# The MLP's product silu(gate)*up made by VectorE from PSUM in a decoder layer

## The chip, the cores and the metric

The kernel runs on one core of a Trainium2 chip. The metric is the device time of one execution in microseconds (us), as the median of several runs; a profile shows one execution instruction by instruction. The engines are TensorE (PE; its weight loads are PEld), VectorE (DVE), ScalarE (ACT) and GpSimd (POOL), with SyncE (SP) issuing the transfers. Each engine runs its own queue in order, and an instruction starts once the semaphores that it names have reached their values.

## What is computed

A decoder layer over x of 8 batches x 256 tokens x 512 features in three residual parts, each followed by a layer norm. Cut to what matters:

```python
# 1: gated linear recurrence
i, f, g = x @ Wi.T, x @ Wf.T, x @ Wg.T
a = sigmoid(f); b = silu(i) * (1 - a)
h = linear_scan(a, b); xg = h * silu(g)
x = layernorm(x + (xg * rsqrt(mean(xg**2) + eps) * w_norm) @ Wo.T)
# 2: WKV recurrence over the keys x and the values ctx, along the tokens
x = layernorm(x + wkv(w, u, k=x, v=ctx))
# 3: MLP, I = 1408, weights and activations rounded to 255 levels by row (quant)
gate, up = quant(x) @ quant(W_gate_up).T          # 1408 columns each
h = silu(gate) * up
x = layernorm(x + quant(h) @ quant(W_down).T)
```

## The kernel before

A batch is two tiles of 128 tokens; tile n = 2b + t is token half t of batch b, 16 tiles in all. The first part of the time loads, rounds and turns the weights. Then the three parts are overlapped across batches: one pass of the loop (`iteration(b, par)`, passes b = 1 to 5) does the MLP of batch b, the WKV part of batch b+1 and the gated recurrence of batch b+2. Batch 0's MLP stands before the loop, those of batches 6 and 7 after it. Nothing schedules the instructions: each engine's `iteration` is an order written out by hand, with semaphores between the engines.

The MLP of a tile is cut in three chunks c of 512, 512 and 384 columns (`CHUNKS`). For each:

- `mlp_up` (TensorE, L557) multiplies into a slot of PSUM, `slot_ps[:, s]`, the gate in its first bank and up in its second. There are two slots, s = (t + c) % 2.
- `scale_products` (VectorE) multiplies the gate by the weights' scales into `gate_buf` (L1522, counted by `gate_scaled`) and up by its scales into `hid_buf(t)` (L1525, counted by `mlp_read`). Both buffers are rows of `ring` in SBUF. After the second the slot is free.
- `silu` (ScalarE, L867) works in place in `gate_buf`.
- `hidden` (GpSimd, L1189) multiplies `hid_buf` by `gate_buf` in place and counts `hid_ready`.
- `hidden_max` (VectorE, L1534) takes the row's largest magnitude; after the third chunk `hidden_scale` derives the scale.

Then `round_hidden` (ScalarE), `turn_hidden` (TensorE, L577, transposes into slot (t+1+NC) % 2), `read_hidden` (ScalarE, into `hqT`), `mlp_down` (TensorE, L590, into slot (t+NC) % 2), `read_down` (VectorE, L1567), `residual_3` (GpSimd, L1194) and layer norm.

TensorE's uses of the slots wait by the count `mlp_read`: `mlp_up`'s chunk 2 for the same tile's chunk 0; `turn_hidden(n)` for tile n+1's chunk 1 (L574, `chunks_read(n) - 1`); `mlp_down(n)` for tile n+1's chunk 2 (L586, `chunks_read(n)`). In a pass TensorE's queue goes, in its second half: `mlp_up` of tile (b,1) chunk 1 and chunk 2, `turn_values` (L523), `turn_hidden(2b)`, `project_out(b+2, 0)` (L455), `sum_squares(b+2)`, `project_out(b+2, 1)`, `mlp_down(2b)`, `turn_inputs(b+1)` (L532); and the next pass begins with `mlp_up` of batch b+1, which waits for ScalarE's `read_inputs` (L858, `xqT`) of what `turn_inputs` wrote. VectorE's `mean_square(b+2)` (L1384) waits for `sum_squares`, `scale_2(b+1)` stands behind it and gives the scale that ScalarE's `round_2` needs ahead of `turn_inputs`.

## Time and profile before

| | |
|---|---|
| median of 3 runs | 489.2 us (488.76 to 492.02) |
| span of the profiled execution | 485.3 us |
| VectorE busy | 426.4 us, 88% |
| TensorE busy | 376.6 us, 78% |
| ScalarE busy | 290.8 us, 60% |
| GpSimd busy | 277.5 us, 57% |
| `hidden` on GpSimd (L1189) | 66.2 us in 48 instructions |

The page's map of the span in 40 slices shows VectorE at eight or nine tenths of nearly every slice from the middle on. The three stages are the weights (to about 106 us), the overlapped passes (batch 0's MLP from 106 us, the loop's five passes from 156 to 417 us) and the batches 6 and 7 after the loop. A row of a timeline gives start, duration and, in brackets, the engine's idle time ahead of it with what ended it; the row of the next instruction on VectorE often starts 0.08 us before the end of the one ahead. Line numbers are those of the kernel before.

### The profile page before, as it was taken

How to read it: one execution, taken by the hardware profiler on the slowest of the kernel's cores; microseconds unless marked ns; L12 is line 12 of the kernel's file. 1: busy time of each engine (PE TensorE's matmuls, PEld its weight loads, DVE VectorE, ACT ScalarE, POOL GpSimd, SP SyncE). 2: the span in 40 equal slices, each digit the busy share in tenths (PEclk: the TensorE clock that was granted, in tenths of full speed). 3: DMA queues.
4: the chain of work that ended last, by engine and by line, in shares of the span. 5: the costliest groups of instructions: out<-in, count | busy, mean ns of one | idle time of the engine just before them, and what ended most of it. 6: DMA issues, size and time to landing. Idle time of an engine off the chain costs nothing.

```text
span 485.3 us, 7425 instructions
## 1 busy us (share of the span) xinstructions
PE 376.6 (78%) x2484; PEld 285.2 (59%) x2484; DVE 426.4 (88%) x705; ACT 290.8 (60%) x374; POOL 277.5 (57%) x249
## 2 busy tenths in 40 slices
PE   5977972997098995899598977898689959556782
PEld 4965972886064973588365865396459836223331
DVE  3897599848999999989998999799998999999983
ACT  4766673493446965387547864586538654854752
POOL 4546574706836754586365935384558636763643
PEclk8997895999589997999989989899799988976998
DMA  8849441460110010201002010301020101000001
GB/s 312 300 171 141 149 156 53 132 108 35 50 37 1 0 66 1 102 8 54 14 22 88 1 66 0 109 0 65 0 105 3 65 0 42 24 0 22 22 24 66
DMA packets 13340, 31.70 MB, mean 65 GB/s; under 512 B 4864, under 2 KB 4864, under 8 KB 13312
## 3 DMA queue, kind: packets, MB, share of 16 engines
q1 hardware_dynamic: 13312, 31.35, 20.4%
q8 instruction: 15, 0.25, 0.2%
q14 instruction: 13, 0.11, 0.1%
HBM read 27.14 MB, written 4.21 MB: 65 GB/s over the span
## 4 chain that ended last, share of the span: by engine, by line
DVE 45%; PE 17%; issue 16%; POOL 9%; DMA 8%; ACT 4%; DVEq 1%; POOLq 0%; SPq 0%; ACTq 0%
DVE q_state L1427 7%; PE proj_ps L455 6%; PE slot_ps L557 6%; DVE p_state L1439 6%; DVE hid_max L1534 4%; DMA ring<-w_gate_up_dram 3%; POOL q_state L1173 2%; DVE ring L1522 2%; DVE ring L1525 2%; DVE num L1447 2%; DVE row_max L1591 2%; DVE inp L1359 2%; POOL ring L1189 2%; POOL z L1194 2%; PE slot_ps L590 2%
## 5 line engine op out<-in xcount | busy, mean ns | idle before, releaser
L557 PE MATMUL slot_ps<-w1q,xqT 128*128 128x512 bf16 (+1 forms) x384 | 88.2, 382 | 20.6 <-DVE z L1567 12.9
L1189 POOL TENSOR_TENSOR ring<-ring 128x512 f32<-128x512 f32 (+1 forms) x48 | 66.2, 1386 | 18.8 <-ACT ring L867 18.7
L557 PEld LDWEIGHTS slot_ps<-w1q,xqT 128*128 128x128 bf16 x384 | 37.8, 102 | 63.8 <-issue 14.5
L455 PE MATMUL proj_ps<-x_high,proj_high 128*128 128x256 f32 x384 | 64.3, 289 | 5.0 <-DVE proj_low L1350 1.9
L455 PE MATMUL proj_ps<-x_high,proj_low 128*128 128x256 f32 x384 | 61.5, 282 | 0.0
L455 PE MATMUL proj_ps<-x_low,proj_high 128*128 128x256 f32 x384 | 61.1, 281 | 0.0
L455 PEld LDWEIGHTS proj_ps<-x_high,proj_high 128*128 128x128 f32 x384 | 52.9, 189 | 7.8 <-issue 6.0
L867 ACT ACTIVATE ring<-ring,zero_bias,x_scale 128x512 f32<-128x512 f32 (+1 forms) x48 | 36.9, 772 | 31.7 <-DVE ring L1522 31.6
L455 PEld LDWEIGHTS proj_ps<-x_high,proj_low 128*128 128x128 f32 x384 | 52.6, 190 | 0.0
L455 PEld LDWEIGHTS proj_ps<-x_low,proj_high 128*128 128x128 f32 x384 | 52.4, 190 | 0.0
L523 PE MATMUL turn_ps<-identity,num 128*128 128x128 f32 x64 | 14.5, 391 | 44.2 <-DVE num L1465 44.2
L1194 POOL TENSOR_TENSOR z<-z,x 128x512 f32<-128x512 f32 x16 | 22.4, 1398 | 44.5 <-DVE z L1567 44.5
L874 ACT ACTIVATE ring<-ring,round_bias,hid_inv 128x768 f32<-128x768 f32 (+1 forms) x32 | 30.2, 967 | 25.9 <-DVE hid_inv L1556 25.9
L590 PE MATMUL slot_ps<-w2q,hqT 128*128 128x512 bf16 x176 | 41.9, 388 | 4.0 <-ACT hqT L881 3.1
L1522 DVE TENSOR_TENSOR ring<-slot_ps,scale_rows 128x512 f32<-128x512 f32 (+1 forms) x48 | 30.7, 640 | 13.3 <-PE slot_ps L557 13.3
L1122 POOL TENSOR_SCALAR ring<-ring,row_inv 128x512 f32<-128x512 f32 (+1 forms) x26 | 28.3, 1100 | 19.1 <-DVE row_inv L1597 19.1
L523 PEld LDWEIGHTS turn_ps<-identity,num 128*128 128x128 f32 x64 | 10.6, 197 | 47.6 <-DVE num L1465 47.4
L1439 DVE TENSOR_TENSOR_SCAN p_state<-decay_col,p_state 128x256 f32<-128x256 f32 x32 | 34.4, 1118 | 4.1 <-POOL p_state L1151 4.0
L1427 DVE TENSOR_TENSOR_SCAN q_state<-decay_col,q_state 128x256 f32<-128x256 f32 x32 | 36.8, 1209 | 0.0
L1151 POOL TENSOR_TENSOR p_state<-q_state,c_sb 128x512 f32<-128x512 f32 x16 | 21.0, 1312 | 20.0 <-ACT q_state L822 11.3
L590 PEld LDWEIGHTS slot_ps<-w2q,hqT 128*128 128x128 bf16 x176 | 16.2, 99 | 24.7 <-issue 5.6
L1591 DVE TENSOR_REDUCE row_max<-ring 128x2 f32<-128x1024 f32 (+1 forms) x15 | 19.7, 1316 | 12.3 <-DMA ring<-w_gate_up_dram 11.4
(115 smaller groups left out, 904.7 us busy)
## 6 DMA issues: line engine op xcount, KB each, us to landing
ring<-w_gate_up_dram SPq DMA_DIRECT2D x11, 512.0 KB, 4.9
forget<-xT_dram SPq DMA_DIRECT2D x8, 512.0 KB, 3.3
x_sb<-x_dram SPq DMA_DIRECT2D x8, 512.0 KB, 3.4
c_sb<-cT_dram SPq DMA_DIRECT2D x8, 512.0 KB, 4.9
out_dram<-z SPq DMA_DIRECT2D x16, 256.0 KB, 2.1
ring<-w_down_dram SPq DMA_DIRECT2D x4, 704.0 KB, 5.0
x<-wfT_dram SPq DMA_DIRECT2D x2, 512.0 KB, 5.0
x<-woT_dram SPq DMA_DIRECT2D x2, 512.0 KB, 4.6
```

The costliest lines, as they stand in the source:

```text
L455: last = nc.tensor.matmul(out, a, b, start=(i == 0), stop=(i == len(terms) - 1))
L557: last = nc.tensor.matmul(slot_ps[:, s, half * 512:half * 512 + width], xqT[:, par, d, t * P:(t + 1) * P], w1q[:, d, half * I + at:half * ...
L590: last = nc.tensor.matmul(slot_ps[:, s, 0:D], hqT[:, i, :], w2q[:, i, :], start=(i == 0), stop=(i == IB - 1))
L867: nc.scalar.activation(g, g, ACT.Silu, bias=zero_bias[:, :], scale=x2_scale[:, par, t:t + 1]).then_inc(silu_ready, 1)
L874: nc.scalar.activation(h, h, ACT.Identity, bias=round_bias[:, :], scale=hid_inv[:, t:t + 1]).then_inc(hid_rounded, 1)
L1122: last = nc.gpsimd.tensor_scalar(rows[:, a, :], rows[:, a, :], row_inv[:, c:c + 1], ROUND, ALU.mult, ALU.add)
L1189: nc.gpsimd.tensor_tensor(hid, hid, gate_buf[:, at:at + width], ALU.mult).then_inc(hid_ready, 1)
L1194: nc.gpsimd.tensor_tensor(z3[:, t, :], z3[:, t, :], x2[:, par, t, :], ALU.add).then_inc(z3_ready, 1)
L1427: last = nc.vector.tensor_tensor_scan(e_past[:, c, :], decay_col[:, c:c + 1].to_broadcast([P, T]), e_past[:, c, :], 0.0, ALU.mult, ALU.add)
L1439: last = nc.vector.tensor_tensor_scan(ev_past[:, c, :], decay_col[:, c:c + 1].to_broadcast([P, T]), ev_past[:, c, :], 0.0, ALU.mult, ALU.add)
L1522: nc.vector.tensor_tensor(gate_buf[:, at:at + width], slot_ps[:, s, 0:width], scale_rows[:, at:at + width], ALU.mult).then_inc(gate_scaled, 1)
L1591: nc.vector.tensor_reduce(row_max[:, cols], rows, AX.X, ALU.max, apply_absolute_value=True).then_inc(row_max_ready, 1)
```

## The change

The product moves from GpSimd to VectorE. `scale_products` now writes the scaled up half back into its PSUM slot and counts `up_scaled`. A new VectorE step `hidden` reads that slot and `gate_buf` and writes `hid_buf`; it counts `mlp_read`, so that the slot is free, by every wait on `mlp_read`, after the product and no longer after the scaling. `hidden_max` waits on `mlp_read`. GpSimd's `hidden` and its 48 calls are gone. The new calls are placed by hand in VectorE's order, a few other VectorE steps change places, and ScalarE does one `silu` ahead of `read_hidden` in two places outside the loop.

```diff
-                        wait(dve, hid_ready, n * NC)
-                        wait(dve, hq_turned, 2 * n - 2)
+                        wait(dve, mlp_read, n * NC)
...
-                    nc.vector.tensor_tensor(hid_buf(t)[:, at:at + width],
+                    nc.vector.tensor_tensor(slot_ps[:, s, 512:512 + width],
                                             slot_ps[:, s, 512:512 + width],
                                             scale_rows[:, I + at:I + at + width],
-                                            ALU.mult).then_inc(mlp_read, 1)
+                                            ALU.mult).then_inc(up_scaled, 1)
+
+            def hidden(b, t, c):
+                n = b * TB + t
+                at, width = CHUNKS[c]
+                s = (t + c) % 2
+                dve.wait_ge(silu_ready, n * NC + c + 1)
+                dve.wait_ge(up_scaled, n * NC + c + 1)
+                if c == 0:
+                    wait(dve, hq_turned, 2 * n - 2)
+                nc.vector.tensor_tensor(hid_buf(t)[:, at:at + width],
+                                        slot_ps[:, s, 512:512 + width],
+                                        gate_buf[:, at:at + width],
+                                        ALU.mult).then_inc(mlp_read, 1)
...
@@ -1608,20 +1586,23 @@
                 n = b * TB
                 scale_products(b, 0, [0])
                 scale_products(b, 0, [1])
-                scale_products(b, 0, [2])
                 hidden_max(b - 1, 1, 0)
                 hidden_max(b - 1, 1, 1)
                 hidden_max(b - 1, 1, 2)
+                hidden(b, 0, 0)
+                hidden_scale(b - 1, 1 - par, 1)
                 sum_values(b + 1, 0)
-                hidden_scale(b - 1, 1 - par, 1)
+                scale_products(b, 0, [2])
                 numerator(b + 1, 0)
                 hidden_max(b, 0, 0)
                 layer_norm_3(n - 2, 0)
+                hidden(b, 0, 1)
                 hidden_max(b, 0, 1)
                 sum_weights(b + 1, 0)
                 sum_weights(b + 1, 1)
+                normalise_3(n - 2, 0)
+                hidden(b, 0, 2)
                 hidden_max(b, 0, 2)
-                normalise_3(n - 2, 0)
...
                 refine(b + 1, 0)
                 refine(b + 1, 1)
+                hidden(b, 1, 0)
                 gating(b + 2)
                 scale_products(b, 1, [1])
...
                 scale_products(b, 1, [2])
+                hidden(b, 1, 1)
                 normalise_2(b + 1, 1 - par)
                 mean_square(b + 2)
                 scale_2(b + 1, 1 - par)
+                hidden(b, 1, 2)
                 normalise_3(n - 1, 1)
```

**VectorE, second half of a pass**, from the `gating` product `inp` to the first `residual_1` (`slot_ps` is the MLP's two slots, `num` the WKV result, `msq` the mean square that TensorE sums). Before:

```order
L1373 TENSOR_TENSOR inp<-inp,gate 128x1024 [waits proj_read]
...
L1522 TENSOR_TENSOR ring<-slot_ps,scale_rows 128x512 [waits mlp_done]
L1525 TENSOR_TENSOR ring<-slot_ps,scale_rows 128x512
L1378 TENSOR_TENSOR xg_low<-inp,xg_high 128x1024 [waits xg_high_ready]
L1471 TENSOR_TENSOR num<-x1,turn_ps 128x512 [waits y_turned] x2
...
L1485 TENSOR_SCALAR ve2<-mv2 128x2 [waits rstd2_ready,mv2_ready]
...
L1522 TENSOR_TENSOR ring<-slot_ps,scale_rows 128x384 [waits mlp_done]
L1525 TENSOR_TENSOR ring<-slot_ps,scale_rows 128x384
L1492 TENSOR_SCALAR x2<-num,mv2,rstd2 128x512 [waits z3_ready,rstd2_ready]
...
L1384 TENSOR_SCALAR msq<-turn_ps 128x2 [waits rms_ready,sumsq_done]
L1499 TENSOR_REDUCE x2_max<-x2 128x2 [waits x2_ready]
```

And after:

```order
L1503 TENSOR_TENSOR ring<-slot_ps,ring 128x512 [waits hq_turned]
...
L1339 TENSOR_TENSOR inp<-inp,gate 128x1024 [waits proj_read]
...
L1487 TENSOR_TENSOR ring<-slot_ps,scale_rows 128x512 [waits mlp_done]
L1490 TENSOR_TENSOR slot_ps<-slot_ps,scale_rows 128x512
L1344 TENSOR_TENSOR xg_low<-inp,xg_high 128x1024 [waits xg_high_ready]
L1437 TENSOR_TENSOR num<-x1,turn_ps 128x512 [waits y_turned] x2
...
L1451 TENSOR_SCALAR ve2<-mv2 128x2 [waits rstd2_ready,mv2_ready]
...
L1490 TENSOR_TENSOR slot_ps<-slot_ps,scale_rows 128x384
L1503 TENSOR_TENSOR ring<-slot_ps,ring 128x512 [waits up_scaled,silu_ready]
...
L1350 TENSOR_SCALAR msq<-turn_ps 128x2 [waits rms_ready,sumsq_done]
...
L1470 TENSOR_SCALAR x2_scale<-x2_max 128x2 [waits hid_inv_ready,silu_ready,x2_max_ready]
...
L1503 TENSOR_TENSOR ring<-slot_ps,ring 128x384 [waits up_scaled,silu_ready]
```

What counts `mlp_read` for chunk 1 was the third row before (L1525, right behind the gating product); now it is the second `ring<-slot_ps,ring 128x512`, behind the split of the states, two residuals, a layer norm's statistics and chunk 2's scaling.

**TensorE, the same half pass**, in the change (its instructions and their waits are the same in both kernels; `w1q` are the up weights, `w2q` the down weights, `xg` the gated states):

```order
L557 MATMUL slot_ps<-w1q,xqT 128x384 [waits mlp_read]
L557 MATMUL slot_ps<-w1q,xqT 128x384 x7
...
L523 MATMUL turn_ps<-identity,num 128x128 [waits e_now_ready,msq_ready,e_past_ready,y_ready]
...
L577 MATMUL slot_ps<-identity16,ring 128x128 [waits mlp_read]
...
L455 MATMUL proj_ps<-wo_high,xg_high 128x512 [waits proj_read]
...
L488 MATMUL turn_ps<-ones,gate 128x1 [waits z2_ready,sq_sum_ready]
...
L590 MATMUL slot_ps<-w2q,hqT 128x512 [waits hq_ready,mlp_read]
...
L532 MATMUL turn_ps<-identity16,num 128x128 [waits z2_ready,x2_rounded]
```

Nothing moved on this queue; what moved is the VectorE instruction that its three waits on `mlp_read` are for.

## Rows read from the trace of the kernel before

**Rows 1.** The page: the span, then busy us (share of the span) xinstructions by engine.

```profile
span 485.3 us, 7425 instructions
...
PE 376.6 (78%) x2484; PEld 285.2 (59%) x2484; DVE 426.4 (88%) x705; ACT 290.8 (60%) x374; POOL 277.5 (57%) x249
```

**Rows 2.** Busy us by engine (x instructions) over the loop's five passes.

```profile
sum 261.20, PE 223.04 PEld 168.83 DVE 245.09 ACT 162.52 POOL 154.81; mean PE 44.61 PEld 33.77 DVE 49.02 ACT 32.50 POOL 30.96
```

**Rows 3.** The page: groups by line, busy us, mean ns | idle us before, releaser.

```profile
L1189 POOL TENSOR_TENSOR ring<-ring 128x512 f32<-128x512 f32 (+1 forms) x48 | 66.2, 1386 | 18.8 <-ACT ring L867 18.7
...
L1522 DVE TENSOR_TENSOR ring<-slot_ps,scale_rows 128x512 f32<-128x512 f32 (+1 forms) x48 | 30.7, 640 | 13.3 <-PE slot_ps L557 13.3
```

**Rows 4.** Timeline, VectorE, first half of pass 3: start us, us, instruction.

```profile
258.22 0.69 DVE L1522 TENSOR_TENSOR ring<-slot_ps,scale_rows 128x512 f32<-128x512 f32 x1 [0.46 <-PE slot_ps L557]
...
269.89 1.15 DVE L1451 COPY num<-c_sb 128x2 f32<-128x2 f32 x1
...
273.30 5.26 DVE L1427 TENSOR_TENSOR_SCAN q_state<-decay_col,q_state 128x256 f32<-128x256 f32 x4
...
278.93 1.28 DVE L1583 TENSOR_SCALAR z<-z,mv,rstd 128x512 f32<-128x512 f32 x1
280.13 1.26 DVE L1439 TENSOR_TENSOR_SCAN p_state<-decay_col,p_state 128x256 f32<-128x256 f32 x2
...
282.95 0.17 DVE L1451 COPY num<-c_sb 128x2 f32<-128x2 f32 x1
...
288.00 0.68 DVE L1522 TENSOR_TENSOR ring<-slot_ps,scale_rows 128x512 f32<-128x512 f32 x1
```

**Rows 5.** Timeline, GpSimd, the same half pass.

```profile
267.63 3.38 POOL L1189 TENSOR_TENSOR ring<-ring 128x512 f32<-128x512 f32 x2
...
273.47 1.33 POOL L1189 TENSOR_TENSOR ring<-ring 128x384 f32<-128x384 f32 x1
274.75 1.66 POOL L1158 TENSOR_TENSOR num<-e_now,c_sb 128x512 f32<-128x512 f32 x1
276.36 1.65 POOL L1164 TENSOR_TENSOR q_state<-q_state,e_now 128x512 f32<-128x512 f32 x1
...
278.64 1.28 POOL L1164 TENSOR_TENSOR q_state<-q_state,e_now 128x512 f32<-128x512 f32 x1
```

**Rows 6.** Timeline, VectorE, second half of that pass.

```profile
295.07 0.68 DVE L1525 TENSOR_TENSOR ring<-slot_ps,scale_rows 128x512 f32<-128x512 f32 x1
...
300.60 0.54 DVE L1525 TENSOR_TENSOR ring<-slot_ps,scale_rows 128x384 f32<-128x384 f32 x1
301.06 1.94 DVE L1492 TENSOR_SCALAR x<-num,mv,rstd 128x512 f32<-128x512 f32 x2
```

**Rows 7.** Timeline, TensorE, second half of that pass [idle before <-releaser].

```profile
287.54 4.88 PE L557 MATMUL slot_ps<-w1q,xqT 128*128 128x512 bf16 x16 [2.45 <-DVE z L1567]
...
295.81 0.79 PE L577 MATMUL slot_ps<-identity,ring 128*128 128x128 f16 x11 [1.68 <-DVE ring L1525]
297.23 1.20 PE L455 MATMUL proj_ps<-wo_high,xg_high 128*128 128x512 f32 x4 [0.63 <-DVE xg_low L1378]
...
303.37 2.55 PE L590 MATMUL slot_ps<-w2q,hqT 128*128 128x512 bf16 x11
306.73 0.62 PE L532 MATMUL turn_ps<-identity,num 128*128 128x128 f16 x8 [0.81 <-ACT num L851]
```

**Rows 8.** Timeline: first up matmuls of pass 3 (TensorE), xqT of pass 4 (ScalarE).

```profile
256.19 3.62 PE L557 MATMUL slot_ps<-w1q,xqT 128*128 128x512 bf16 x16 [1.28 <-ACT xqT L858]
...
307.39 1.11 ACT L858 ACTIVATE xqT<-turn_ps,half_bias 128x1024 bf16<-128x1024 f16 x1 [0.71 <-PE turn_ps L532]
```

**Rows 9.** Busy us by engine in three stretches, granted clock (PEclk), DMA.

```profile
256.00:260.00 4.00, 3.81 (x20) 1.98 (x21) 3.08 (x6) 0.81 (x2) 0.69 (x1) 1.00 0.52 194
287.50:290.90 3.40, 3.36 (x10) 1.34 (x11) 3.40 (x4) 1.96 (x3) 3.33 (x3) 0.60 0.00 0
308.60:312.10 3.50, 3.45 (x9) 1.25 (x10) 1.88 (x4) 1.15 (x1) 1.47 (x2) 0.51 0.59 225
```

**Rows 10.** Timeline, VectorE, end of tile 1, before the loop.

```profile
152.40 3.69 DVE L1416 TENSOR_SCALAR x<-inp,mv,rstd 128x512 f32<-128x512 f32 x2
156.01 0.68 DVE L1522 TENSOR_TENSOR ring<-slot_ps,scale_rows 128x512 f32<-128x512 f32 x1
```

**Rows 11.** Timeline after the loop: TensorE, tiles 12 and 13; VectorE, tile 14.

```profile
446.87 0.77 PE L577 MATMUL slot_ps<-identity,ring 128*128 128x128 f16 x11 [0.17 <-DVE ring L1525]
...
460.25 1.02 PE L590 MATMUL slot_ps<-w2q,hqT 128*128 128x512 bf16 x4 [0.80 <-ACT hqT L881]
...
455.57 0.69 DVE L1522 TENSOR_TENSOR ring<-slot_ps,scale_rows 128x512 f32<-128x512 f32 x1
...
458.44 0.54 DVE L1583 TENSOR_SCALAR z<-z,mv,rstd 128x512 f32<-128x512 f32 x1
```

More of the change, by code:

```diff
@@ L1046, in _ @@
             round_2(1, 1, 1)
+            silu(0, 0, 1, [1])
             read_hidden(0, 0, 0)
             read_hidden(0, 0, 1)
-            silu(0, 0, 1, [1])
             read_inputs(1, 1)
@@ L1080, in _ @@
             round_hidden(12, 0, 1)
+            silu(6, 0, 1, [1])
             read_hidden(12, 0, 0)
             read_hidden(12, 0, 1)
-            silu(6, 0, 1, [1])
             silu(6, 0, 1, [2])
@@ L1180, in rstd_2 @@
                                         ALU.pow).then_inc(rstd2_ready, 1)
-            def hidden(b, t, chunks=range(NC)):
-                n = b * TB + t
-                for c in chunks:
-                    at, width = CHUNKS[c]
-                    pool.wait_ge(silu_ready, n * NC + c + 1)
-                    pool.wait_ge(mlp_read, n * NC + c + 1)
-                    hid = hid_buf(t)[:, at:at + width]
-                    nc.gpsimd.tensor_tensor(hid, hid, gate_buf[:, at:at + width],
-                                            ALU.mult).then_inc(hid_ready, 1)
             def residual_3(n, par, t):
@@ L1208, in iteration @@
                 now_values(b + 1, 0)
-                hidden(b, 0, [0])
-                hidden(b, 0, [1])
                 past_values(b + 1, 1)
                 rstd_3(n - 2, 0)
-                hidden(b, 0, [2])
                 now_values(b + 1, 1)
@@ L1281, in _ @@
             denominator(1, 1)
-            hidden(0, 0, [0])
             newton(1, 0)
             newton(1, 1)
-            hidden(0, 0, [1])
-            hidden(0, 0, [2])
             sum_blocks(2)
@@ L1289, in _ @@
             rms_scale(2)
-            hidden(0, 1, [0])
-            hidden(0, 1, [1])
             rstd_1(2)
-            hidden(0, 1, [2])
             iteration(1, 1)
@@ L1305, in _ @@
             past_values(7, 1)
-            hidden(6, 0, [0])
-            hidden(6, 0, [1])
             now_values(7, 1)
-            hidden(6, 0, [2])
             denominator(7, 0)
@@ L1532, in hidden_max @@
                 at, width = CHUNKS[c]
-                dve.wait_ge(hid_ready, n * NC + c + 1)
+                dve.wait_ge(mlp_read, n * NC + c + 1)
                 nc.vector.tensor_reduce(hid_max[:, c:c + 1], hid_buf(t)[:, at:at + width], AX.X,
@@ L1719, in _ @@
             weigh_inputs(2)
+            hidden(0, 0, 0)
             numerator(1, 1)
@@ L1727, in _ @@
             gating(2)
+            hidden(0, 0, 1)
             residual_2(1, 0)
@@ L1732, in _ @@
             split_states(2)
+            hidden(0, 0, 2)
             hidden_max(0, 0, 2)
@@ L1739, in _ @@
             scale_products(0, 1, [1])
+            hidden(0, 1, 0)
+            scale_products(0, 1, [2])
             mean_square(2)
-            scale_products(0, 1, [2])
+            hidden(0, 1, 1)
             residual_1(2, 0)
             residual_1(2, 1)
+            hidden(0, 1, 2)
             layer_norm_1(2)
@@ L1760, in _ @@
             hidden_scale(5, 1, 1)
-            scale_products(6, 0, [2])
+            hidden(6, 0, 0)
             sum_values(7, 0)
             sum_values(7, 1)
+            scale_products(6, 0, [2])
             numerator(7, 0)
             hidden_max(6, 0, 0)
+            hidden(6, 0, 1)
             sum_weights(7, 0)
@@ L1768, in _ @@
             hidden_max(6, 0, 1)
+            hidden(6, 0, 2)
             hidden_max(6, 0, 2)
@@ L1781, in _ @@
             layer_norm_2(7)
+            hidden(6, 1, 0)
             scale_products(6, 1, [1])
@@ L1785, in _ @@
             scale_2(7, 1)
+            hidden(6, 1, 1)
             layer_norm_3(11, 1)
@@ L1788, in _ @@
             hidden_max(6, 1, 1)
+            hidden(6, 1, 2)
+            hidden_max(6, 1, 2)
             read_down(12, 6, 0)
-            hidden_max(6, 1, 2)
             hidden_scale(6, 0, 1)
@@ L1795, in _ @@
             normalise_3(11, 1)
+            hidden(7, 0, 0)
+            normalise_3(12, 0)
+            hidden(7, 0, 1)
             scale_products(7, 0, [2])
-            normalise_3(12, 0)
             hidden_max(7, 0, 0)
             hidden_max(7, 0, 1)
+            hidden(7, 0, 2)
             hidden_max(7, 0, 2)
@@ L1804, in _ @@
             scale_products(7, 1, [1])
+            hidden(7, 1, 0)
             hidden_max(7, 1, 0)
+            hidden(7, 1, 1)
             scale_products(7, 1, [2])
@@ L1808, in _ @@
             hidden_max(7, 1, 1)
+            hidden(7, 1, 2)
             hidden_max(7, 1, 2)
```

14 lines of the change are left out of this document (1 added, 13 removed).

## The prediction

> **What bounds the kernel now.** The page's first part comes first: VectorE is busy 426.4 of 485.3 us, TensorE 376.6, GpSimd 277.5 [rows 1]. An average hides stages, so the stretches of the loop come next: its five passes last 261.2 us together, 52.2 each, and VectorE is busy 49.0 of a mean pass [rows 2]. In the loop VectorE is the bound, almost without a gap. TensorE waits for it: 2.45 us for `read_down`, then 1.68 us for the scaling of up chunk 1 of the odd tile, which ends at 295.75 (295.07 + 0.68), and `turn_hidden` starts at 295.81 [rows 6, 7]. That last wait is by `mlp_read`, the count whose meaning is changed. From there to the next pass TensorE works through two projections, `mlp_down` and `turn_inputs`, with time left over: `turn_inputs` waits 0.81 us for ScalarE's `num`, which waits for VectorE [rows 7].
>
> **The change: VectorE's time.** 48 instructions leave GpSimd (66.2 us there) and 48 come to VectorE [rows 3]. No row has a product of a PSUM and an SBUF row of `ring`, but the scaling has the same shape, one operand from PSUM and one from SBUF: 0.64 us each in the mean, of which 0.08 lies under the next instruction (300.60 + 0.54 against 301.06) [rows 3, 6]. That makes 48 x 0.56 = 27 us. A pass has six of them, four of 512 columns at 0.60 and two of 384 at 0.46 (300.60 to 301.06): 3.3 us. Writing the scaled row to PSUM in place of SBUF I cost at nothing; no row shows such a write, and a tenth of a microsecond on each of six would be 0.6 us a pass, inside the range.
>
> Something comes back. Instructions on VectorE are held by GpSimd's: the copy of two columns at 269.89 takes 1.15 us and ends at 271.04, where two `hidden` end (267.63 + 3.38 = 271.01); the same copy at 282.95, with GpSimd idle, takes 0.17 [rows 4, 5]. Four scans take 5.26 us beside `hidden` chunk 2, `now_values` and a `denominator`, against 1.26 for two that are free; the normalisation behind them takes 1.28 [rows 4, 5], against 0.54 at 458.44, where it is free [rows 11]; the two at 301.06 take 1.94, so one of those is held too, by about 0.9 [rows 6]. By their GpSimd partners I put down to `hidden` 0.98 (copy), some 0.8 (the first held scan, beside the GpSimd row at 273.47), 0.9 (the pair at 301.06) and, for the small instructions between, an estimated 0.6: 3.3 us a pass. So VectorE's own sum is even: +3.3 - 3.3.
>
> The Trainium skill has a rule for this, SBUF — State Buffer, section "Who interferes with whom": GpSimd and a VectorE instruction with two SBUF inputs, or in a two-port mode, exclude each other for the whole instruction, and one with at most one SBUF input does not contend. The trace agrees with the copy and the scans, and by the rule the new product, one input from PSUM, is not held itself. By it the sum is the even one above.
>
> In the first half of a pass I pushed the rows. Product 0 and `hidden_scale` fall where chunk 2's scaling stood and where VectorE waited; products 1 and 2 add 1.07 us and 0.1 of handoffs; the copy gives back 0.98, and of the 2.8 + 0.74 us that scans and normalisation are held, some 1.9 stay (`now_values` and one `denominator` still run there), so 1.6 goes. Net -1.4: tile (b,1)'s first scaling, 29.8 us behind the pass's first (258.22 to 288.00) [rows 4], comes 28.4 us behind it.
>
> **The change: the slot is held longer.** This decides. `turn_hidden(2b)` waits for tile (b,1)'s chunk 1. Its release was the scaling of up at 295.75. It is now product 1, which stands where the row at 301.06 stands; product 0 ahead of it adds 0.60, its own duration is 0.68, and the -1.4 comes off: 301.06 + 0.60 + 0.68 - 1.4 = 300.9 [rows 6]. The release comes 5.2 us later in the pass, 42.7 us behind the pass's first scaling. (In every other pass the first half is 1.3 us shorter, so I take 42.1.) Queued behind `turn_hidden` on TensorE are both `project_out`, `sum_squares`, `mlp_down` and `turn_inputs`. VectorE itself soon waits for them, at `mean_square`, with `scale_2` behind it, `round_2` behind that.
>
> From the release to the next pass's first scaling, from rows: `turn_hidden` 0.75; projections and sum 303.37 - 297.23 = 6.14; `mlp_down` 2.55; `turn_inputs` 0.62; ScalarE's `xqT` 1.11 [rows 7, 8]; chunk 0's matmuls from their start at 256.19 to the scaling at 258.22, 2.03 [rows 4, 8]; handoffs 0.1. That is 13.3. VectorE's path beside it is shorter. Counted from the release, `msq` runs at +4.2, when `sum_squares` is done; the row scale takes it to +6, product 2 to +6.5 (`mlp_down` could start at +6.9); the residuals, layer norm, `read_down` and `normalise_1` end by +12. So a pass takes 42.1 + 13.3 = 55.4 at the full clock, +3.2 on 52.2.
>
> **TensorE's clock.** After the 2.45 us pause the granted clock is 0.60 in the next 3.4 us, and in another stretch it is 0.51, the 1.2 GHz level: 9 matmuls in 3.45 us, where the full level did 20 in 3.81 [rows 7, 9]. Ahead of the new release TensorE pauses some 5.6 us (the odd tile's chunk 2 and `turn_values` are done by about 295.3). So `turn_hidden` and the first projection fall in a slow stretch of 3.4 us at least; half its work is lost, 1.7 us. Lower bound 0, upper bound 3.4 (two stretches). The skill's TensorE: Matmul & The Clock Gate, Part 1, states the same two levels and that the gate lowers the clock after idleness; this rule speaks against any change that makes TensorE wait. The loop then costs 5 x (3.2 + 1.7) = 24.5 us, from 16 to 33.
>
> **Before and after the loop.** Batch 0: chunk 2 of tile 0 waits for product 0, and the last two `project` behind it on TensorE delay `gating` by 1.7 us; chunk 1 of tile 1 waits for product 2 of tile 0 (0.8 more); `silu` of chunk 2 stands behind `read_hidden`, which waits for product 1, so product 2, `mlp_down` and `read_down` come some 3.5 us late. Against them the normalisation at 152.40, 3.69 us long where about 1.0 is free, is no longer held [rows 10]. Pushed through, the first scaling of pass 1 moves from 156.0 to 160 or 162: +5, from 2 to 7.
>
> Batches 6 and 7: `turn_hidden(12)`, at 446.87, moves behind product 1 of tile 13, +4.6, and `mlp_down(12)` behind product 2, whose `silu` stands behind `read_hidden`, +0.9; 1.0 less from scans no longer held: +4.5. Tile 14: `mlp_down(13)` started 4.7 us behind the tile's first scaling (455.57 to 460.25) [rows 11]; it now needs product 2, which by the new order ends at about +8: +3. Tile 15 has the same shape but ends in the row scale: +2. Together +9.5, from 5 to 12.
>
> **Sum.** 24.5 + 5 + 9.5 = 39 us on the profiled 485.3, or 524.3. The median of the runs is 3.9 above that execution, so 528.2; the terms' ends give 23 to 52, so 512 to 541.
>
> **Rivals.**
> - *No change.* VectorE stays the bound, the sum of its time is even, and TensorE's later start is absorbed: 489 (484 to 494). For it: [rows 2], and the gain in the first half. Against it: a chain of 13.3 us behind a release 42.1 us into a pass of 52.2 doesn't fit, by 3.2. It decides if the release comes that much earlier or the chain is that much shorter. 4%.
> - *Faster.* More comes back than I count: if all 48 `hidden` held VectorE for their 1.39 us, 66 us would come back for 27. It decides once more than 27 us come back and the chain fits: 2 us a pass less, 479. By the Trainium skill's GPSIMD Engine Reference, section 4.1, elementwise work with two inputs belongs on VectorE, being about twice as fast there; the rows have 1.39 against 0.64 [rows 3]. Against it: GpSimd isn't the bound, and [rows 4] shows less than 3.5 us a pass held by `hidden`. 3%.
> - *VectorE's time alone.* It stays the bound and nothing comes back: 489.2 + 27 = 516. The held instructions would have to be held as long by what GpSimd still does. 8%.
> - *The chain with a slow clock throughout*, both projections and `mlp_down` at the lower level: 4 us more a pass, 548. 7%.
> - *My forecast*, the later release: 78%.
>
> **How the numbers follow.** The time is the sum, 528. The range 512 to 541 takes in the terms' ends and the rival at 516. About 1% is what a measurement of this kernel tells from no change: faster 0.03, same 0.04, slower 0.93.
>
> **What would show it.** In the profile after: passes of 56 to 58 us; VectorE's busy share down to about 82%, with a new wait of 3 to 5 us at `msq` for TensorE's `turn_ps`; TensorE idle 5 to 6 us ahead of `turn_hidden`, released by the new product; a granted clock near 0.5 behind it; the copies at 0.17 us more often. Wrong would be: a `turn_hidden` released by something other than the product; a pass under 54 us (the chain has slack that I don't see); products held by GpSimd, well over 0.68 us each.

## The result and the profile after

The changed kernel takes 539.6 us (median; 537.8 to 540.9), the kernel before 490.6 beside it: ratio 1.101 (1.095 to 1.106), 49 us slower. Line numbers are now those of the changed kernel: L1487 and L1490 scale gate and up, L1503 is the product, L1350 `mean_square`, L1545 `read_down`. The page's head, and groups with the idle time before them and its releaser:

```profile
span 538.0 us, 7379 instructions
...
PE 383.9 (71%) x2462; PEld 294.1 (55%) x2484; DVE 423.9 (79%) x753; ACT 291.6 (54%) x374; POOL 212.6 (40%) x201
...
L557 PE MATMUL slot_ps<-w1q,xqT 128*128 128x512 bf16 (+1 forms) x377 | 86.6, 378 | 61.4 <-DVE ring L1503 53.4
...
L577 PE MATMUL slot_ps<-identity,ring 128*128 128x128 f16 x176 | 16.7, 261 | 39.4 <-DVE ring L1503 38.5
L1503 DVE TENSOR_TENSOR ring<-slot_ps,ring 128x512 f32<-128x512 f32 (+1 forms) x48 | 30.7, 639 | 4.6 <-ACT ring L867 4.6
```

VectorE has 48 instructions more and is busy 2.5 us less than before [rows 1]; they cost 30.7 us and more than that came back. But its share falls from 88 to 79 per cent: it now waits. TensorE is idle for 92 us (53.4 + 38.5) in these two groups until a product frees a slot, where it was idle for 33 us (20.6 + 12.4) ahead of the same two before, for any reason:

```profile
L557 PE MATMUL slot_ps<-w1q,xqT 128*128 128x512 bf16 (+1 forms) x384 | 88.2, 382 | 20.6 <-DVE z L1567 12.9 <-ACT xqT L858 7.6
...
L577 PE MATMUL slot_ps<-identity,ring 128*128 128x128 f16 x176 | 15.6, 245 | 12.4 <-DVE ring L1525 6.9 <-ACT ring L874 4.6 <-DVE z L1567 0.8
```

VectorE in pass 3 (start, duration, instruction, idle time before it with its releaser):

```profile
280.29 0.69 DVE L1487 TENSOR_TENSOR ring<-slot_ps,scale_rows 128x512 f32<-128x512 f32 x1 [1.42 <-PE slot_ps L557]
...
290.53 0.17 DVE L1417 COPY num<-c_sb 128x2 f32<-128x2 f32 x1
...
294.31 3.49 DVE L1393 TENSOR_TENSOR_SCAN q_state<-decay_col,q_state 128x256 f32<-128x256 f32 x4
...
307.14 0.69 DVE L1487 TENSOR_TENSOR ring<-slot_ps,scale_rows 128x512 f32<-128x512 f32 x1
...
320.68 0.68 DVE L1503 TENSOR_TENSOR ring<-slot_ps,ring 128x512 f32<-128x512 f32 x1
321.28 1.00 DVE L1458 TENSOR_SCALAR x<-num,mv,rstd 128x512 f32<-128x512 f32 x2
327.94 0.16 DVE L1350 TENSOR_SCALAR msq<-turn_ps 128x2 f32<-128x2 f32 x1 [5.66 <-PE turn_ps L488]
...
336.87 0.69 DVE L1487 TENSOR_TENSOR ring<-slot_ps,scale_rows 128x512 f32<-128x512 f32 x1 [1.44 <-PE slot_ps L557]
```

And TensorE behind the release at 321.36 (320.68 + 0.68):

```profile
321.42 1.35 PE L577 MATMUL slot_ps<-identity,ring 128*128 128x128 f16 x11 [5.85 <-DVE ring L1503]
322.53 2.05 PE L455 MATMUL proj_ps<-wo_high,xg_high 128*128 128x512 f32 x4
...
327.77 1.17 PE L455 MATMUL proj_ps<-wo_high,xg_high 128*128 128x512 f32 x4
```

The pass is 56.6 us long: 41.1 to the release, 15.5 from there to the next pass's first scaling. `turn_hidden` took 0.79 for the same 11 matmuls in pass 3 before [rows 7]; here it and most of the first projection run at half speed. The windows of the two stretches (columns as in rows 9; the last but two is the granted clock) show that it is the clock:

```profile
321.40:326.90 5.50, 5.48 (x21) 4.56 (x22) 0.88 (x2) 2.18 (x3) 0.00 (x0) 0.50 0.00 0
327.00:334.00 7.00, 6.57 (x37) 4.35 (x36) 5.85 (x14) 1.84 (x3) 0.99 (x2) 1.00 0.28 88
```

The half clock itself is not new. Rows 7 show the one pass of the kernel before in which this work ran at full speed; in the other four it took the same 1.33 to 1.36 and 2.05 to 2.07 us as here. Its pass 4:

```profile
348.64 1.35 PE L577 MATMUL slot_ps<-identity,ring 128*128 128x128 f16 x11 [1.22 <-DVE ring L1525]
350.06 2.07 PE L455 MATMUL proj_ps<-wo_high,xg_high 128*128 128x512 f32 x4
```

What is new is that the pass now waits behind it, as e5_busy and e7_before_busy show below.

Cut at the first scaling of a batch, the time of each kernel's profiled execution divides as follows. "Batch 0" is from the first scaling of all to that of pass 1, "pass" the mean of the loop's five, then batch 6 to batch 7, and batch 7 to the end of VectorE's last instruction.

Each ratio is to runs of the kernel before on the same chip at the same time.

| kernel | median, us | ratio to before | batch 0 | pass | b6 to b7 | b7 to end |
|---|---|---|---|---|---|---|
| before | 490.6 | | 50.1 | 52.3 | 38.3 | 27.0 |
| the change | 539.6 | 1.101 (1.095 to 1.106) | 58.5 | 56.3 | 46.9 | 38.0 |
| e1_sbuf | 504.6 | 1.032 (1.027 to 1.036) | 51.5 | 52.7 | 42.2 | 32.6 |
| e2_sbuf_late | 549.5 | 1.124 (1.119 to 1.128) | 58.6 | 58.6 | 47.7 | 36.8 |
| e3_pe_order | 521.5 | 1.068 (1.062 to 1.073) | 58.4 | 53.9 | 46.9 | 34.2 |
| e5_busy | 521.7 | 1.068 (1.060 to 1.075) | 57.9 | 54.2 | 44.6 | 33.4 |
| e6_place | 519.5 | 1.062 (1.057 to 1.067) | 58.7 | 51.7 | 47.1 | 36.7 |
| e7_before_busy | 490.7 | 1.000 (0.997 to 1.003) | 50.4 | 52.1 | 37.7 | 27.0 |
| e8_orders | 506.5 | 1.032 (1.028 to 1.037) | 56.1 | 50.9 | 46.5 | 36.8 |
| e9_order_alone | 494.9 | 1.010 (1.006 to 1.014) | 51.3 | 51.9 | 40.2 | 29.0 |
| e10_loop_only | 487.1 | 0.993 (0.990 to 0.997) | 50.7 | 51.4 | 38.6 | 26.8 |
| e11_orders_before | 501.8 | 1.026 (1.022 to 1.031) | 50.7 | 54.1 | 38.6 | 27.0 |

So the change costs 8.5 us in batch 0, 19.9 in the loop and 19.6 behind it. The stretch ahead of the first scaling, where the change alters nothing, took 105.9 us in the profiled execution of before and 108 to 111 in all others; together with the 1.8 us by which a span is shorter than the time of the same execution, that accounts for this span, 485.3, lying below the median. The last stretch also varies: the change, e3_pe_order and e6_place have the same instructions in it, and it took 38.0, 34.2 and 36.7 us. The granted clock over it was 0.86, 0.95 and 0.86. Differences of a few us there are not an experiment's doing by this table alone.

### The profile page after: what moved, and what is told of

It reads as the page before. It is cut to its first block, busy times and chain, and to the rows that moved or that the text cites. A ratio compares the mean times of both kernels' runs of the same rounds, so it can differ in the third digit from the quotient of the medians.

```text
span 538.0 us, 7379 instructions
## 1 busy us (share of the span) xinstructions
PE 383.9 (71%) x2462; PEld 294.1 (55%) x2484; DVE 423.9 (79%) x753; ACT 291.6 (54%) x374; POOL 212.6 (40%) x201
## 3 DMA queue, kind: packets, MB, share of 16 engines
q1 hardware_dynamic: 13312, 31.35, 19.6%
## 4 chain that ended last, share of the span: by engine, by line
DVE 39%; PE 30%; issue 14%; DMA 7%; ACT 5%; POOL 4%; DVEq 1%; POOLq 0%; SPq 0%; ACTq 0%
PE proj_ps L455 14%; PE slot_ps L557 8%; DVE q_state L1393 5%; PE slot_ps L590 5%; DVE ring L1503 4%; DMA ring<-w_gate_up_dram 4%; DVE p_state L1405 4%; DVE slot_ps L1490 3%; DVE hid_max L1512 3%; DVE num L1431 2%; DVE inp L1325 2%; DVE row_max L1569 2%; DVE ring L1487 2%; DVE stats L1443 2%; PE slot_ps L577 2%
## 5 line engine op out<-in xcount | busy, mean ns | idle before, releaser
L557 PE MATMUL slot_ps<-w1q,xqT 128*128 128x512 bf16 (+1 forms) x377 | 86.6, 378 | 61.4 <-DVE ring L1503 53.4
L455 PE MATMUL proj_ps<-x_high,proj_high 128*128 128x256 f32 x384 | 68.1, 301 | 6.6 <-DVE inp L1358 4.8
L455 PEld LDWEIGHTS proj_ps<-x_high,proj_high 128*128 128x128 f32 x384 | 56.7, 202 | 9.2 <-issue 7.7
L590 PE MATMUL slot_ps<-w2q,hqT 128*128 128x512 bf16 x161 | 46.1, 442 | 16.1 <-DVE ring L1503 12.2
L455 PEld LDWEIGHTS proj_ps<-x_high,proj_low 128*128 128x128 f32 x384 | 54.8, 198 | 0.0
L881 ACT ACTIVATE hqT<-slot_ps,half_bias 128x768 bf16<-128x768 f16 (+1 forms) x32 | 25.4, 842 | 41.8 <-PE slot_ps L577 41.8
L1487 DVE TENSOR_TENSOR ring<-slot_ps,scale_rows 128x512 f32<-128x512 f32 (+1 forms) x48 | 30.6, 638 | 18.1 <-PE slot_ps L557 17.9
L577 PE MATMUL slot_ps<-identity,ring 128*128 128x128 f16 x176 | 16.7, 261 | 39.4 <-DVE ring L1503 38.5
L577 PEld LDWEIGHTS slot_ps<-identity,ring 128*128 128x128 f16 x176 | 13.6, 119 | 43.2 <-DVE ring L1503 24.3
L1503 DVE TENSOR_TENSOR ring<-slot_ps,ring 128x512 f32<-128x512 f32 (+1 forms) x48 | 30.7, 639 | 4.6 <-ACT ring L867 4.6
L1405 DVE TENSOR_TENSOR_SCAN p_state<-decay_col,p_state 128x256 f32<-128x256 f32 x32 | 30.6, 998 | 4.6 <-POOL p_state L1151 4.6
L1164 POOL TENSOR_TENSOR q_state<-q_state,e_now 128x512 f32<-128x512 f32 x16 | 24.7, 1545 | 19.2 <-DVE q_state L1393 18.6
```

Source lines behind the costliest of these rows:

```text
L455: last = nc.tensor.matmul(out, a, b, start=(i == 0), stop=(i == len(terms) - 1))
L557: last = nc.tensor.matmul(slot_ps[:, s, half * 512:half * 512 + width], xqT[:, par, d, t * P:(t + 1) * P], w1q[:, d, half * I + at:half * ...
L577: last = nc.tensor.transpose(part_16(s, part)[:, i * P:(i + 1) * P], low_halves(hid_buf(t)[:, (first + i) * P: (first + i + 1) * P]), iden ...
L590: last = nc.tensor.matmul(slot_ps[:, s, 0:D], hqT[:, i, :], w2q[:, i, :], start=(i == 0), stop=(i == IB - 1))
L1405: last = nc.vector.tensor_tensor_scan(ev_past[:, c, :], decay_col[:, c:c + 1].to_broadcast([P, T]), ev_past[:, c, :], 0.0, ALU.mult, ALU.add)
L1487: nc.vector.tensor_tensor(gate_buf[:, at:at + width], slot_ps[:, s, 0:width], scale_rows[:, at:at + width], ALU.mult).then_inc(gate_scaled, 1)
```

## The experiments

Two theories stood against each other. H: the held slot, and TensorE's queue behind it, make the time. V: VectorE's own 48 instructions make it.

### e1_sbuf: the slot released by the scaling

```diff
-                    nc.vector.tensor_tensor(slot_ps[:, s, 512:512 + width],
+                    nc.vector.tensor_tensor(hid_buf(t)[:, at:at + width],
                                             slot_ps[:, s, 512:512 + width],
                                             scale_rows[:, I + at:I + at + width],
-                                            ALU.mult).then_inc(up_scaled, 1)
+                                            ALU.mult).then_inc(mlp_read, 1)
...
                 nc.vector.tensor_tensor(hid_buf(t)[:, at:at + width],
-                                        slot_ps[:, s, 512:512 + width],
+                                        hid_buf(t)[:, at:at + width],
                                         gate_buf[:, at:at + width],
-                                        ALU.mult).then_inc(mlp_read, 1)
+                                        ALU.mult).then_inc(hid_ready, 1)
```

> The changed kernel with one thing undone: the scaled up half is written to its SBUF row again, its instruction frees the slot as before the change, and VectorE's product reads two SBUF rows. Product, place and count of VectorE instructions are those of the change. Theory H (the slot is held to the product, and TensorE's queue waits): the waits of turn_hidden and mlp_down on the product go, passes return from 56.2 to about 52, time 487 to 502. Rival V (VectorE's 30.7 us of products are the cost): 515 or more.

Measured: 504.6 us, just above H's range and far from V's; passes of 52.7. Every order is that of the changed kernel, VectorE makes all 48 products, and its busy time is even higher than in the changed kernel:

```profile
PE 379.0 (75%) x2462; PEld 289.1 (57%) x2484; DVE 438.8 (87%) x753; ACT 291.5 (58%) x374; POOL 217.3 (43%) x201
```

35 of the 49 us are gone. V falls as the main cause.

### e2_sbuf_late: the same with the late release

e1_sbuf, with TensorE's four waits for a slot on the product's count:

```diff
-                pe.wait_ge(mlp_read, chunks_read(n) - 1)
+                pe.wait_ge(hid_ready, chunks_read(n) - 1)
```

> As e1_sbuf, but TensorE's four waits for a free slot are on the count of the product again; nothing else differs from e1_sbuf, on no engine. Theory H: 535 to 545, passes of 56, the idle time ahead of turn_hidden back. Rival V: as e1_sbuf. Rival P (writing and reading the scaled row in PSUM is what costs): as e1_sbuf, well under the change's 539.6.

Measured: 549.5 us. These waits alone are worth 45 us, on the same instructions, and rival P falls. That H expected less is the other result: with both operands in SBUF the kernel is 10 us slower than with one in PSUM, 549.5 against 539.6. The trace's row for the product's line, first here, then in the changed kernel (ns: shortest/median/longest):

```profile
L1501 DVE TENSOR_TENSOR ring<-ring x48: 548/682/1728, 128.8 to 532.2; 128x512 f32<-128x512 f32 x32, 128x384 f32<-128x384 f32 x16
```

```profile
L1503 DVE TENSOR_TENSOR ring<-slot_ps,ring x48: 541/680/693, 129.3 to 520.7; 128x512 f32<-128x512 f32 x32, 128x384 f32<-128x384 f32 x16
```

The medians agree; only the SBUF product is ever held, up to 1.73 us, as here beside GpSimd (a free one of 384 columns takes 0.55):

```profile
305.47 1.52 POOL L1164 TENSOR_TENSOR q_state<-q_state,e_now 128x512 f32<-128x512 f32 x1
305.75 1.66 DVE L1501 TENSOR_TENSOR ring<-ring 128x384 f32<-128x384 f32 x1
```

In sum it is 41.7 against 30.7 us, 11 us, and VectorE's busy time differs by that (435.0 against 423.9). One operand in PSUM kept all 48 free. So the rule of the Trainium skill's SBUF — State Buffer, section "Who interferes with whom", that an instruction with at most one SBUF input does not contend with GpSimd, agrees with these rows.

### e3_pe_order: other work ahead of the wait

In the loop TensorE does both projections and the sum of squares before the `turn_hidden` that waits:

```diff
-                turn_hidden(n, 0, 0)
-                turn_hidden(n, 0, 1)
                 project_out(b + 2, 0)
                 sum_squares(b + 2)
                 project_out(b + 2, 1)
+                turn_hidden(n, 0, 0)
+                turn_hidden(n, 0, 1)
                 mlp_down(n, 0)
```

> The change, with TensorE's order altered in the loop alone: both project_out and sum_squares ahead of turn_hidden of the even tile. Theory H: TensorE does its 6.1 us of projections in the 5.85 us that it waits, the 5.66 us wait at msq goes, passes fall from 56.2 to 51 or 52, time 510 to 520. Rival V: no change, 540, since VectorE has the same work.

Measured: 521.5 us, passes of 53.9, both a little above H's ranges. What was queued behind the wait carried over half of its cost in the loop (12 of 20 us). The other 6 us by which this run is faster lie outside the loop, where nothing was changed: 3.8 in the last stretch, 2.4 ahead of the first scaling. What is left of the loop's cost shows in these rows of pass 3:

```profile
320.55 0.56 DVE L1503 TENSOR_TENSOR ring<-slot_ps,ring 128x384 f32<-128x384 f32 x1 [2.37 <-ACT ring L867]
321.39 3.47 PE L590 MATMUL slot_ps<-w2q,hqT 128*128 128x512 bf16 x10 [2.81 <-DVE ring L1503]
```

Product 2 now waits for ScalarE's `silu`, which stands behind `read_hidden` on ScalarE's queue, and `mlp_down` waits for product 2 and then runs slowly.

### e5_busy: spare matmuls in the waits

Matmuls whose result nobody reads fill TensorE's waits, 24 ahead of `turn_hidden(2b)` in each pass and 6 to 14 at ten waits behind the loop:

```diff
+                pe.wait_ge(proj_read, (b + 2) * PROJ + 5)
+                keep_busy(24)
                 turn_hidden(n, 0, 0)
```

> The change, with spare matmuls on TensorE (bf16, 512 columns, into a free bank of proj_ps) in the stretches in which it waits for products: 24 ahead of turn_hidden in a pass, 6 to 14 ahead of ten waits behind the loop. They keep it busy and should end before the wait does. Theory C (2 us a pass and half of what is lost behind the loop come from the half clock that follows the wait): the chain from the release to the next pass falls from 15.5 to about 13.3 us, behind the loop 5 to 9 us less, time 520 to 530. Rival (the waits alone cost, the clock nothing): 538 to 545.

Measured: 521.7 us, 18 less than the change, with the late release untouched. In every pass `turn_hidden` now takes 0.77 to 0.79 and the projection's first four matmuls 1.18; pass 3:

```profile
309.08 5.34 PE L615 MATMUL proj_ps<-w2q 128*128 128x512 bf16 x24
315.08 0.79 PE L577 MATMUL slot_ps<-identity,ring 128*128 128x128 f16 x11 [0.66 <-DVE ring L1521]
315.68 1.18 PE L455 MATMUL proj_ps<-wo_high,xg_high 128*128 128x512 f32 x4
```

A pass is 2.0 us shorter, the stretches behind the loop 2.3 and 4.6, together 17 us. Of the last 4.6 it is open how much the spare matmuls made, since e3_pe_order has 3.8 less there without them. The 18 us are 3.3% of the time. The Trainium skill's TensorE: Matmul & The Clock Gate, Part 1, puts the penalty of the ramp, the slow start of a kernel's matmuls, at under 1% of a typical kernel's span; this kernel falls back to the lower clock in every pass, and the measured price is higher.

### e7_before_busy: the control

The same on the kernel before: 8 spare matmuls in a pass, and 8, 12 and 34 in the long waits behind the loop.

> Control for the clock: the kernel before, with spare matmuls in the waits that its TensorE has itself: 8 of 512 columns ahead of turn_hidden(2b) in each pass, and 8, 12 and 34 in the three long waits behind the loop. The result is not touched. P (the half clock costs only where TensorE's chain sets the pass): in the kernel before VectorE is the bound of the loop, so the spare matmuls bring nothing there and at most the half clock of 434 to 445 us behind it, 485 to 490. G (the gain of 18 us that spare matmuls brought in the changed kernel is one that any version of this kernel would get): 475 or less.

Measured: 490.7 us, ratio 1.000 (0.997 to 1.003), just above P's range and far from G's. The spare matmuls did lift the clock: `turn_hidden` took 0.77 to 0.79 us in all five passes, and the mean granted clock rose from 0.93 to 0.97 in the loop and from 0.82 to 0.95 between batches 6 and 7. So in this kernel the half clock cost nothing where TensorE isn't on the path; the 18 us of e5_busy are a price of the change and no gain that lay there before.

### e6_place: one call moved

```diff
                 residual_2(b + 1, 0)
                 residual_2(b + 1, 1)
+                hidden(b, 1, 1)
                 layer_norm_2(b + 1)
                 scale_products(b, 1, [2])
-                hidden(b, 1, 1)
                 normalise_2(b + 1, 1 - par)
```

> The changed kernel with one call moved on VectorE's queue in the loop: product 1 of the odd tile, hidden(b, 1, 1), stands right behind the two residuals instead of behind the layer norm's statistics and chunk 2's scaling. Nothing else is changed. R (the release decides): that product frees the slot for turn_hidden(2b), so the release comes earlier by what stood between, the statistics of two halves and the two scalings of chunk 2, some 2.7 us. The chain behind the release is 15.5 us whatever stands ahead of it, so each of five passes is 2 to 2.7 us shorter: 526 to 530. V (VectorE's own time decides): its instructions are the same and so is the time, 538 to 541.

Measured: 519.5 us, 20 less than the change, more than R expected and far from V. VectorE, then TensorE, in a pass that begins at 272.84 and ends at 324.10:

```profile
310.41 0.68 DVE L1503 TENSOR_TENSOR ring<-slot_ps,ring 128x512 f32<-128x512 f32 x1
...
315.17 0.16 DVE L1350 TENSOR_SCALAR msq<-turn_ps 128x2 f32<-128x2 f32 x1 [0.47 <-PE turn_ps L488]
...
324.10 0.69 DVE L1487 TENSOR_TENSOR ring<-slot_ps,scale_rows 128x512 f32<-128x512 f32 x1 [1.44 <-PE slot_ps L557]
```

```profile
311.15 0.79 PE L577 MATMUL slot_ps<-identity,ring 128*128 128x128 f16 x11 [3.02 <-DVE ring L1503]
311.75 1.18 PE L455 MATMUL proj_ps<-wo_high,xg_high 128*128 128x512 f32 x4
...
311.10:316.60 5.50, 5.45 (x34) 4.64 (x35) 4.86 (x12) 2.30 (x3) 2.19 (x4) 1.00 0.00 0
```

(The last line is the window behind the release.) The release comes 38.3 us into the pass (311.09 - 272.84), 2.8 earlier than in the change, as R had it. The chain behind it is 13.0 us instead of 15.5, since the matmuls behind the wait of 3.02 us ran at the full clock in four of the five passes, where those behind 5.85 ran at half; R had left that out. 38.3 + 13.0 is the pass of 51.3. One call in the wrong place made the whole loss in the loop: the mean pass is now 51.7, no longer than before. (The profiled execution was the fastest of four, 515.9.)

### e8_orders: three orders put right

e6_place, with e3_pe_order's edit and ScalarE's `silu` ahead of `read_hidden`, this in the loop and also in batches 0 and 6:

```diff
                 silu(b, par, 1, [1])
+                silu(b, par, 1, [2])
                 read_hidden(n, 0, 0)
                 read_hidden(n, 0, 1)
-                silu(b, par, 1, [2])
```

> The changed kernel, its product still made from PSUM, with three orders put right at once: TensorE's two turn_hidden(2b) in the loop stand behind the projections (as in the run e3_pe_order, 521.5 us), ScalarE's silu of the odd tile's chunk 2 stands ahead of read_hidden (in the loop, in batch 0 and in batch 6), and VectorE's product 1 stands right behind the residuals. R: in e3_pe_order product 2 waited 2.0 to 2.4 us for that silu and mlp_down 2.8 us for the product; without these waits a pass is 1 to 1.6 us shorter than its 53.9, near the 52.3 of the kernel before, and batches 0 and 6 gain 1 to 2 us each: 508 to 517. V: VectorE's time sets the pass at 53.9 already: 518 to 524.

Measured: 506.5 us, a little below R's range. Passes of 50.9 us, 1.3 less than before; the loss outside the loop stays, 6.0 + 8.2 + 9.7 us.

### e9_order_alone: the moves without the product

The kernel before, with the changed kernel's other moves of steps on VectorE and ScalarE. In the loop:

```diff
                 scale_products(b, 0, [1])
-                scale_products(b, 0, [2])
...
-                sum_values(b + 1, 0)
                 hidden_scale(b - 1, 1 - par, 1)
+                sum_values(b + 1, 0)
+                scale_products(b, 0, [2])
                 numerator(b + 1, 0)
...
+                normalise_3(n - 2, 0)
                 hidden_max(b, 0, 2)
-                normalise_3(n - 2, 0)
```

> The kernel before with only the changed kernel's other moves: on VectorE the scaling of chunk 2 of the even tile behind hidden_scale and sum_values, normalise_3 ahead of hidden_max, and the like outside the loop; on ScalarE the two silu ahead of read_hidden. The product stays on GpSimd. It splits the 16 us that remained in e1_sbuf (504.6 us, the slot released early). Q (the moves are worth nothing or little by themselves, and the 16 us are the product's own time on VectorE): 487 to 494. O (the moves delay chunk 2's release and what hangs on it): 498 to 506.

Measured: 494.9 us, ratio 1.010 (1.006 to 1.014), just above Q's range: the moves by themselves cost 5 us by the medians. By the stretches they cost 1.2 us in batch 0 and 3.9 behind the loop, and the loop is 1.7 us shorter (passes of 51.9). By subtraction, not by a run of its own, some 11 us of e1_sbuf's 16 are the product's own time on VectorE, held instructions included.

### e10_loop_only and e11_orders_before: product and orders apart

e10_loop_only takes e8_orders' loop and the kernel before outside it. One function decides for a batch:

```diff
+        def on_pool(b):
+            return isinstance(b, int) and b in (0, 6, 7)
...
+                    if on_pool(b):
+                        nc.vector.tensor_tensor(hid_buf(t)[:, at:at + width],
+                                                slot_ps[:, s, 512:512 + width],
+                                                scale_rows[:, I + at:I + at + width],
+                                                ALU.mult).then_inc(mlp_read, 1)
+                    else:
+                        nc.vector.tensor_tensor(slot_ps[:, s, 512:512 + width],
+                                                slot_ps[:, s, 512:512 + width],
+                                                scale_rows[:, I + at:I + at + width],
+                                                ALU.mult).then_inc(up_scaled, 1)
```

> The product is made by VectorE from PSUM in the loop's ten tiles alone, with the three orders of e8_orders; the MLPs of batches 0, 6 and 7 are those of the kernel before, instruction and order (VectorE scales up into the SBUF row, GpSimd makes the product, the scaling frees the slot). L (the costs outside the loop and the gain inside it are apart): e8_orders had passes of 50.9 us against 52.3 of the kernel before, 6.6 us in five passes, and all its loss outside them; so 480 to 486. M (the loss outside comes with the loop's own ends, or the pass is bound by what batch 0 leaves late): 488 to 498.

e11_orders_before is the kernel before with e3_pe_order's edit and the `silu` move in the loop.

> Control for e10_loop_only: the kernel before, product on GpSimd, with the two orders of the other queues in the loop: TensorE's turn_hidden(2b) behind the projections, ScalarE's silu of the odd tile's chunk 2 ahead of read_hidden. If VectorE is the bound of the loop (its 49.0 busy of 52.2 us), TensorE's and ScalarE's orders bring nothing: 487 to 492. If the gain of e8_orders' passes lies in these orders and not in the product: 481 to 485.

Measured: e10_loop_only 487.1 us, ratio 0.993 (0.990 to 0.997), faster than both kernels, by little and outside the noise, though between L and M. Passes of 51.4 gain 4 us in the loop, and outside it the stretches are back at 50.7, 38.6 and 26.8. e11_orders_before fell outside both expectations: 501.8 us, 2.6% slower. The two orders, made together, do harm without the product on VectorE. TensorE in its pass 3, and the window of the first stretch:

```profile
306.65 2.07 PE L455 MATMUL proj_ps<-wo_high,xg_high 128*128 128x512 f32 x4 [2.52 <-DVE xg_low L1378]
...
312.64 1.20 PE L455 MATMUL proj_ps<-wo_high,xg_high 128*128 128x512 f32 x4
...
317.36 2.32 PE L590 MATMUL slot_ps<-w2q,hqT 128*128 128x512 bf16 x10 [1.02 <-ACT hqT L881]
...
306.60:312.30 5.70, 5.65 (x15) 4.51 (x15) 5.53 (x11) 1.01 (x2) 5.52 (x6) 0.50 0.00 0
```

The first projection starts 37.7 us into the pass, as in pass 4 of the kernel before (350.06 - 312.36). There `turn_hidden` was done by then, in the time that TensorE now waits for VectorE's split (2.52 us). Here it comes later, 0.79 us, and `mlp_down` waits 1.02 for what ScalarE reads of it. The half clock lasts longer too: the second projection starts 5.99 us behind the first, against 4.59. These three make 3.2 us, and this pass takes 54.5 against that one's 51.5. In the same place e8_orders waits less and runs at full speed:

```profile
304.39 1.19 PE L455 MATMUL proj_ps<-wo_high,xg_high 128*128 128x512 f32 x4 [1.41 <-DVE xg_low L1344]
```

So the gain of e10_loop_only isn't that of the orders on TensorE and ScalarE alone. How it divides between the product, these orders and VectorE's moved steps is open: the moves alone already give passes of 51.9 (e9_order_alone). Whether the product with one call placed well and the other queues as they were would do as well in the loop wasn't run by itself with the old batches 0, 6 and 7.

## Why the prediction was right, step by step

**Direction and mechanism held.** `turn_hidden` is released by the product after 5.85 us of idleness ("5 to 6" on record), VectorE's new wait is at `msq` (5.66; 3 to 5 on record), its share fell to 79 per cent (82), the two-column copy shown takes 0.17, the clock behind the release is 0.50. e2_sbuf_late against e1_sbuf shows the release as the cause: 45 us by four waits.

**The total had luck.** Only the loop's term lies within its own range. Batch 0 cost 8.5 us where 2 to 7 stood, the stretches behind the loop 19.6 where 5 to 12 stood; the loop, 4.6 us cheaper than said, took back a third of that. The kernel before also has a median of 490.6 us in these runs where the sum started from 489.2. Without that partial offset 539.6 would have been outside 512 to 541.

**VectorE's own sum.** The even sum was near: +30.7 us of products, busy time -2.5. Over the loop it was better than even, 237.6 us busy against 245.2 before, 1.5 a pass. More came back in the first half of a pass than I pushed through: -2.9 us (26.85 against 29.78) and not -1.4; the four scans take 3.49 where 5.26 stood [rows 4]. The write into PSUM that I costed at nothing costs nothing:

```profile
L1490 DVE TENSOR_TENSOR slot_ps<-slot_ps,scale_rows x48: 548/685/692, 111.2 to 518.6; 128x512 f32<-128x512 f32 x32, 128x384 f32<-128x384 f32 x16
```

**The loop: 24.5 us predicted, 19.9 measured.** The release comes 41.1 us into pass 3 (42.7 predicted) and the chain is 15.5 (13.3 + 1.7 = 15.0). Both parts of that chain were shown apart: 13.0 in pass 3 of e6_place and of e5_busy, at the full clock, so 2.5 for the clock there and 2.0 in e5_busy's mean pass. The half clock was not new, though: four of the five passes before had it, and [rows 7] are of the fifth. It had lain in slack, and the later release put it on the path. The mis-sized part was the first half of a pass, taken 1.5 us too long: more came back, and 42.1 counts the first half as 1.3 us shorter in every second pass only, where the trace before has it shorter in four of five (28.1 to 28.5 against 29.8), which gives 41.7.

**Before the loop: 5 predicted, 8.5 measured.** The chain named was right, and each link longer: product 2 waits for `silu`, then TensorE waits and runs at half speed, then VectorE waits for it. VectorE, then TensorE:

```profile
162.68 0.56 DVE L1503 TENSOR_TENSOR ring<-slot_ps,ring 128x384 f32<-128x384 f32 x1 [2.21 <-ACT ring L867]
...
167.51 0.75 DVE L1545 SCALAR_TENSOR_TENSOR z<-slot_ps,hid_scale,scale_rows 128x512 f32<-128x512 f32 x1 [2.54 <-PE slot_ps L590]
```

```profile
163.69 3.71 PE L590 MATMUL slot_ps<-w2q,hqT 128*128 128x512 bf16 x10 [3.54 <-DVE ring L1503]
```

**After the loop: 9.5 predicted, 19.6 measured.** This is the term that failed, and it makes most of the distance from 528 to 539.6. I counted only how much later the releases come, +4.5, +3 and +2, and left two things out. One is the clock, which I had counted in the loop alone. TensorE waits 2 to 4 us ahead of most groups there, and `mlp_down` of tiles 12 and 13 nearly doubles:

```profile
461.38 1.33 PE L577 MATMUL slot_ps<-identity,ring 128*128 128x128 f16 x11 [4.00 <-DVE ring L1503]
466.10 4.40 PE L590 MATMUL slot_ps<-w2q,hqT 128*128 128x512 bf16 x10 [3.38 <-DVE ring L1503]
...
488.82 4.47 PE L590 MATMUL slot_ps<-w2q,hqT 128*128 128x512 bf16 x10 [2.73 <-DVE ring L1503]
```

It took 2.55 before [rows 7]. e5_busy gives 6.9 us back here, 2.3 of it between batches 6 and 7 and 4.6 in the last stretch, of which up to 3.8 may be chance. The other is the moved steps, which cost 3.9 us here by themselves (e9_order_alone) and which I had taken for nothing. 9.5 + 6.9 + 3.9 = 20.3, near the 19.6; the two experiments don't start from the same kernel and each stretch is of one execution, so this sum is a check and no proof.

**The rivals.** "VectorE's time alone", 516, fell with e1_sbuf. "A slow clock throughout" had too long a slow stretch for the loop (the second projection is at full speed again, 1.17), and was near what happened behind it. "No change" needed the release or the chain 3.2 us shorter; e6_place's 2.8 and the clock did that. "Faster" was nearer than I thought, though not by its mechanism: with the same product and another order the loop's passes are 0.6 to 1.3 us shorter than before in single executions, and e10_loop_only's median confirms 4 us in all. In the loop the change as made is slower because of where its calls stand and what its count means, not because VectorE makes the product. Outside the loop that is not shown: e8_orders still loses 24 us there, and even with the early release e1_sbuf takes 42.2 and 32.6 us behind the loop, where the moves alone take 40.2 and 29.0.

## What to carry to other kernels

When work moves onto an engine, ask first what its completion now releases, and where in the queue that instruction stands: here one call two steps too late cost the loop all that it lost, while the 30 instructions added in it cost it nothing. A buffer's release should be counted by its last necessary reader and that reader placed by who waits, or the value be moved out of the scarce buffer first. A later release of TensorE is to be priced twice, once for the wait and once for the matmuls behind it at the lower clock, in every stage and not only in the loop. And before one pass serves as the baseline, the others should be looked at: here the one that was read was the only one at full speed.
